# Pre-norm attention and expert block on one core: the query and key projections as three f32r products with split operands

## The reference, cut to what matters

```python
x = x + attn(layernorm(x))      # causal, window 128, 16 heads of 8
x = x + moe(layernorm(x))       # 16 experts, 4 chosen per token, and a shared one
# in attn:
qkv = x @ w_in.T + b_in         # the query and key parts of this are what changes
scores = einsum('bhqd,bhkd->bhqk', q, k) / sqrt(8), masked, softmax, @ v
return out @ w_out.T + b_out
```

## Time and profile before

| what | value |
|---|---|
| median of 3 runs (lowest to highest) | 761.21 us (756.61 to 762.22) |
| time of the profiled execution | 758.62 us |
| its span in the trace | 756.8 us |
| granted TensorE clock over the span | 0.972 |
| TensorE, matmul busy | 706.9 us (93%) |
| VectorE busy | 585.8 us (77%) |
| ScalarE busy | 362.4 us (48%) |
| GpSimd busy | 306.4 us (40%) |

### The profile page before, as it was taken

One profiled execution on the slowest core, in us unless ns is written; L12 is line 12 of the kernel. 1 busy time (PEld: TensorE's weight loads), 2 busy tenths in 40 slices (PEclk: granted clock), 3 DMA queues, 4 the chain that ended last, 5 costly groups with the idle time before them and its releaser, 6 DMA issues.

```text
span 756.8 us, 21746 instructions
## 1 busy us (share of the span) xinstructions
PE 706.9 (93%) x8499; PEld 472.2 (62%) x8499; DVE 585.8 (77%) x1741; ACT 362.4 (48%) x739; POOL 306.4 (40%) x327
## 2 busy tenths in 40 slices
PE   4597999999999999999778999999999999999997
PEld 2365666666666666666555666666666666666664
DVE  6776788888888888888577878887777888777632
ACT  2165566767776676667562332333333233333321
POOL 6410221222211222122215656566666656664543
PEclk9589899999999999999999999999999999999999
DMA  2125123333323222333118366654445666544550
GB/s 59 58 87 148 62 85 102 102 102 102 101 61 101 86 70 93 102 102 101 59 35 207 73 138 154 155 134 113 118 122 137 152 155 120 131 103 108 119 139 29
DMA packets 64837, 79.96 MB, mean 106 GB/s; under 512 B 10960, under 2 KB 38880, under 8 KB 64736
## 3 DMA queue, kind: packets, MB, share of 16 engines
q1 hardware_dynamic: 64736, 78.58, 39.9%
HBM read 61.00 MB, written 17.56 MB: 104 GB/s over the span
## 4 chain that ended last, share of the span: by engine, by line
PE 80%; DVE 7%; DMA 5%; ACT 4%; issue 2%; SPq 1%; POOL 1%; DVEq 0%; ACTq 0%; PEldq 0%
PE ps_c L1571 14%; PE ps_att L1356 7%; PE ps_sc L1330 6%; PE ps_max L1288 5%; PE ps_max L1560 4%; PE ps_max L1562 4%; PE ps_max L1561 4%; PE ps_sc L1306 4%; PE ps_sc L1561 4%; PE ps_sc L1562 4%; PE ps_sc L1560 4%; PE ps_a L1254 3%; ACT probs L683 3%; PE ps_c L1574 2%; PE ps_b L1247 2%
## 5 line engine op out<-in xcount | busy, mean ns | idle before, releaser
L618 POOL TENSOR_TENSOR probs<-probs,stacks 128x512 f32<-128x512 f32 x128 | 165.0, 1290 | 125.7 <-DVE probs L1105 75.4
L775 ACT ACTIVATE probs<-ps_max 128x512 f32<-128x512 f32 x144 | 86.2, 598 | 220.1 <-PE ps_max L1562 216.5
L886 DVE TENSOR_REDUCE chunkmax<-ps_max 128x16 f32<-128x512 f32 (+1 forms) x256 | 155.3, 648 | 37.9 <-PE ps_max L1269 37.8
L683 ACT ACTIVATE probs<-ps_sc 128x512 f32<-128x512 f32 x256 | 138.9, 595 | 48.6 <-PE ps_sc L1306 47.6
L1105 DVE TENSOR_TENSOR probs<-probs,ps_sc 128x512 f32<-128x512 f32 x128 | 87.3, 682 | 69.6 <-PE ps_sc L1562 26.4
L1571 PE MATMUL ps_c<-probs,wd 128*128 128x512 f32 x256 | 130.3, 592 | 1.3 <-POOL probs L618 1.3
L1560 PE MATMUL ps_max<-xh,whigh 128*128 128x512 f32 x144 | 93.7, 650 | 2.9 <-DVE probs L1105 2.1
L531 POOL TENSOR_TENSOR xres<-xin,cvec 128x512 f32<-128x512 f32 x16 | 20.6, 1287 | 141.1 <-DVE x L938 140.7
L1330 PE MATMUL ps_sc<-stacks 32*64 32x192 f16 (+2 forms) x2048 | 64.4, 232 | 9.5 <-ACT probs L683 2.7
L1356 PE MATMUL ps_att<-probs,stacks 128*32 128x192 f32 (+1 forms) x1536 | 70.2, 317 | 0.0
L1288 PE MATMUL ps_max<-hl,qdiag 32*128 32x160 f16 (+4 forms) x1024 | 50.9, 220 | 16.0 <-DVE chunkmax L886 9.7
(11 more groups left out here) (164 smaller groups left out, 1257.1 us busy)
## 6 DMA issues: line engine op xcount, KB each, us to landing
stacks<-weight_scratch SPq DMA_DIRECT2D x32, 1024.0 KB, 10.0
stacks<-qk_scratch SPq DMA_DIRECT2D x48, 256.0 KB, 3.4
qk_scratch<-hl SPq DMA_DIRECT2D x32, 256.0 KB, 3.4
xin<-in_L_attn_x_dram SPq DMA_DIRECT2D x16, 256.0 KB, 3.1
x_scratch<-x SPq DMA_DIRECT2D x16, 256.0 KB, 2.2
xin<-x_scratch SPq DMA_DIRECT2D x16, 256.0 KB, 8.9
xres<-x_scratch SPq DMA_DIRECT2D x16, 256.0 KB, 8.9
out_dram<-result SPq DMA_DIRECT2D x16, 256.0 KB, 8.8
```

The lines of the kernel that those rows point to most:

```text
L618: nc.gpsimd.tensor_tensor(inter[p % 3], gated[p % 2], spread[d % 2][:, p, :], ALU.mult).then_inc(inter_ready, 1)
L683: nc.scalar.activation(dst[:, :], ps_sc[s][:, 0:dst.shape[1]], ACT.Exp, scale=SCALE).then_inc(probs_ready, 1)
L775: nc.scalar.activation(silu[n % 2][rows, :], ps_max[n % 2][rows, :], ACT.Silu).then_inc(silu_ready, 1)
L886: nc.vector.tensor_reduce(chunkmax[:, 2 * pair + m, at:at + CHUNKS[h]], ps_max[m][:, 0:BANK_COLS[h]].rearrange("p (n k) -> p n k", k=KB), ...
```

## The change

Two pieces of split data are added: `xT` gets a high part `xT_high` and a low part `xT_low` (both 128x512, f32r), and the query and key weights get `wqk_high` and `wqk_low` (128x256, f32r). From step 1 on, a projection is the sum of three f32r products (high x high, low x high, high x low) in the same bank. Step 0 stays as it was. The parts are made so:

- ScalarE copies the transposed block a second time, from `ps_a` to `xT_high`, right behind the copy to `xT`. `project_v` now waits for this copy too.
- POOL subtracts `xT_high` from `xT` (`low_xT(i + 1)`), behind `layer_norm(i + 1)` and ahead of `residual(i + 1)`. TensorE waits for it in each of the two projections.
- Once, in `body(0)`, ScalarE copies the weights to `wqk_high` behind its copies of block 1. POOL makes `wqk_low` from it ahead of `other_constants`, and TensorE waits for it ahead of `body(1)`.

```diff
@@ POOL
+            def low_xT(d):
+                if not valid(d):
+                    return
+                pool.wait_ge(xT_high_ready, d)
+                after(pool, qk_done, 2 * d if d > 1 else 0)
+                nc.gpsimd.tensor_tensor(xT_low[:, :], xT[:, :], xT_high[:, :].bitcast(FP32), ALU.subtract
+                                        ).then_inc(xT_low_ready, 1)
+
+            def low_wqk():
+                pool.wait_ge(wqk_high_ready, 1)
+                nc.gpsimd.tensor_tensor(wqk_low[:, :, :], wT[:, 0:2, :], wqk_high[:, :, :].bitcast(FP32), ALU.subtract
+                                        ).then_inc(wqk_low_ready, 1)
             for i in range(STEPS):
                 residual(i)
                 if i == 0:
                     clear()
                 layer_norm(i + 1)
                 if i == 0:
+                    low_wqk()
                     other_constants()
+                low_xT(i + 1)
@@ ACT
                 nc.scalar.copy(xT[:, :], ps_a[:, :]).then_inc(xT_ready, 1)
+                if d > 0:
+                    nc.scalar.copy(xT_high[:, :], ps_a[:, :]).then_inc(xT_high_ready, 1)
...
                 transpose_out(prep + 1)
+                if prep == 0:
+                    act.wait_ge(wt_ready, 1)
+                    nc.scalar.copy(wqk_high[:, :, :], wT[:, 0:2, :]).then_inc(wqk_high_ready, 1)
                 take_att(now, 1)
@@ PE
-                mm((ps_b, ps_c)[n][:, :], wT[:, n, :], xT[:, :], start=True, stop=True).then_inc(qk_done, 1)
+                bank = (ps_b, ps_c)[n]
+                if d == 0:
+                    last = mm(bank[:, :], wT[:, n, :], xT[:, :], start=True, stop=True)
+                else:
+                    pe.wait_ge(xT_low_ready, d)
+                    mm(bank[:, :], wqk_high[:, n, :], xT_high[:, :], start=True, stop=False)
+                    mm(bank[:, :], wqk_low[:, n, :], xT_high[:, :], start=False, stop=False)
+                    last = mm(bank[:, :], wqk_high[:, n, :], xT_low[:, :], start=False, stop=True)
+                last.then_inc(qk_done, 1)
...
                 pe.wait_ge(xT_ready, d + 1)
+                after(pe, xT_high_ready, d)
...
             body(0)
             pe.wait_ge(consts2_ready, 1)
+            pe.wait_ge(wqk_low_ready, 1)
```

More of the change, by code:

```diff
@@ L105, in build_block @@
         xT = sb("xT", [P, TOK], FP32)
+        xT_high = sb("xT_high", [P, TOK], F32R)
+        xT_low = sb("xT_low", [P, TOK], F32R)
+        wqk_high = sb("wqk_high", [P, 2, P], F32R)
+        wqk_low = sb("wqk_low", [P, 2, P], F32R)
         hl = sb("hl", [P, 2, 2, TOK], FP16)
@@ L224, in build_block @@
         xT_ready = sem("xT_ready")
+        xT_high_ready = sem("xT_high_ready")
+        xT_low_ready = sem("xT_low_ready")
+        wqk_high_ready = sem("wqk_high_ready")
+        wqk_low_ready = sem("wqk_low_ready")
         qk_done = sem("qk_done")
```

## The result

The changed kernel took 766.75 us (median of 22 runs, 761.89 to 772.46), the kernel before 762.25 in 22 runs beside it (756.61 to 765.46): a ratio of 1.0064, 95% interval 1.0045 to 1.0084. The change costs 0.6%, where the prediction had 760.0 against the profiled execution of before, or 762.6 against the median shown. 766.75 lies outside both of its ranges (756.5 to 764, and 755 to 765.5 for 80%). That the ratio would be within 1% of no change was right, but the prediction held that less than about 1% couldn't be told from none, and 22 runs of each told 0.6%.

A forecast was written before the change was run, and what follows sets the result against it. It took ScalarE and then VectorE to hold the settled step, with projections as filler. From 758.62 us, +1.85 at the start and -0.5 in step 1 gave 760.0; own range 756.5 to 764, 80% range 755 to 765.5.

The forecast's parts named there:

- The projections are filler beside ScalarE's work: Settled attention step: `scores 2` and `scores 3` start 0.05 us behind ScalarE's exponentials, so the projections do not set the time.
- The shorter products: Projections on TensorE: three f32r products at 0.23 us replace one of 0.86, saving 0.16 us each, 4.8 over 15 steps.
- ScalarE's second copy: Behind the first copy in each step: ends 0.50 us later, taken as cost 0, bounds 0 and 0.1 a step.
- GpSimd's subtraction: `low_xT` in each step: 1.3 us long (bounds 1.0 and 2.6), 1.7 us of slack before `project_qk 0`, cost 0.
- VectorE held by the subtraction: Rival: GpSimd's subtraction slows VectorE or pushes L531 along `spread_q`, up to 0.94 us a step, 774 us; chance 0.04.
- The start, +1.85: `body(1)` on TensorE starts at 37.15 instead of 35.30 us, behind `low_wqk` and the constants; bounds 1.3 and 2.3.
- Step 1, -0.5: First step with f32r projections, at half clock and without `take_attn`: savings count, -0.5 us, ends -0.2 and -0.7.
- The clock "rises at the same moment / after as much work": TensorE's clock from `body(1)`: up to -0.9 us if same moment, 0 if after as much dense work; 0 taken.
- the zero case: TensorE's clock rises after as much dense work as before, adding 0 us.
- 0 for the 14 settled steps: Settled attention steps: ScalarE and then VectorE hold the step, so TensorE's savings gain 0; at most 0.6 us in all.
- the sum: Whole kernel: +1.85 us at the start, -0.5 in step 1, 0 in the settled steps, added to 758.62.
- the two 1% marks: Whole kernel: faster by over 1% (under 751 us) chance 0.02, slower by over 1% (over 768.8) chance 0.05.

The follow-up runs named there:

- h3: Changed kernel with projections left as one float32 product and four satisfied waits added in each projection; 766.53 us, ratio 1.0076 to the kernel before.
- h4: Kernel before with only the change's start: weight copy, `low_wqk` ahead of the constants and TensorE's wait; 761.12 us, ratio 1.0013.
- h2: Changed kernel run again unchanged, on another chip, against the kernel before; 769.08 us, ratio 1.0067.
- e1_same: Kernel before, nothing changed, against itself; 763.74 us, ratio 1.0013.
- h5: Kernel before with the change's start and sixteen satisfied waits more a step, nothing else of the change; 764.59 us, ratio 1.0053.
- g1: Changed kernel with `low_wqk` behind the constants, fewer waits, and 192 do-nothing instructions once in TensorE's `body(0)`; 760.53 us, ratio 0.9958 to the kernel before.
- g2: Changed kernel with `low_wqk` behind the constants and fewer waits, without the 192 do-nothing instructions; 771.13 us, ratio 1.0113 to the kernel before.
- h6: Kernel before with sixteen satisfied waits (eight instructions) more a TensorE step, repeated on another chip; 764.11 us, ratio 1.0042.
- h1: Kernel before with sixteen satisfied waits (eight instructions) more a TensorE step, first run; 764.78 us, ratio 1.0009.
- e2: Kernel before with the four new tensors allocated and not used; 764.21 us, ratio 1.0035.
- e4: Changed kernel with each projection left as one float32 product, the split operands made and not used; 772.24 us, ratio 1.010 to the kernel before.
- f1: Changed kernel with float32 projections, plus 192 do-nothing instructions once in TensorE's `body(0)`; 762.57 us, ratio 0.9966 to the kernel before.
- f4: Kernel before with 192 do-nothing instructions once in TensorE's `body(0)`; 766.42 us, ratio 1.0042.

## Why the prediction was wrong, step by step

- **"The projections are filler beside ScalarE's work"**: right. `scores 2` stands at 1.89 behind the transposes in both traces, and in on-time steps the step is 21.05 in both. h3 against after confirms it from the other side.
- **"The shorter products", 0.16 us each:** right (0.23 apart), and lost, as said.
- **ScalarE's second copy** at 0: right; it lasts 0.62 and ends at `take_att`'s start. **GpSimd's subtraction** at 1.3 us and no cost: right (1264 ns, mean of 15; 1.69 us of slack where 1.7 was worked out).
- **VectorE held by the subtraction:** did not happen; the two reductions beside it last 692 and 682 ns where they had 692 and 681, and the floor of the step is unchanged. The Trainium skill's "GPSIMD Engine Reference" (the table of its first section, row "SBUF interfaces") ties the contention to the kind of VectorE instruction. The trace agrees for these reductions, which read PSUM.
- **The start, +1.85:** nearly right, +2.10. GpSimd's row says why:

```profile
33.68 0.72 POOL L610 TENSOR_TENSOR wqk_low<-wT,wqk_high 128x256 fp32r<-128x256 f32 x1 [2.97 <-ACT wqk_high L763]
...
36.68 0.62 POOL L493 TENSOR_SCALAR_AFFINE_SELECT edges<-edges 64x64 bf16<-64x64 bf16 x2
```
```profile
37.40 0.64 PE L1369 MATMUL ps_sc<-stacks 32*64 32x192 f16 x12 [2.07 <-POOLq L587]
```

  TensorE waits 2.07 us for GpSimd. The subtraction took 0.72 (0.7 was estimated), the constants end at 37.30 (37.15), and 0.4 of the shift is not the change's at all: `spread_q` of step 0 took 7.50 us instead of 7.08, and all that follows was later. h4's start, 0.86 later than before, shows how much run-to-run movement lies in that term.
- **Step 1, -0.5:** about right. `scores 2` came 1.58 us behind the projection's start (42.22 - 40.64) where it was 2.00, 0.4 less; up to the anchor 0.3 of it were left.
- **The clock "rises at the same moment / after as much work":** taken as 0. Busy time by stretch, after and then before, of TensorE's time at the 1.2 GHz level (a clock of 0.50):

```profile
17.30:44.60 27.30, 14.21 (x175) 9.82 (x176) 19.50 (x51) 6.79 (x14) 12.62 (x23) 0.50 0.13 41
...
37.40:44.60 7.20, 7.20 (x73) 4.59 (x74) 3.64 (x15) 3.94 (x7) 3.14 (x6) 0.50 0.01 1
```
```profile
18.20:42.10 23.90, 13.80 (x173) 8.86 (x174) 17.40 (x47) 5.41 (x12) 10.17 (x21) 0.50 0.15 46
```

  It rose 2.5 us later with a `body(1)` that began 2.1 later, after 7.20 us of its work where before had 6.80: nearly the zero case. What the prediction did not price is the clock's next drop, in step 1: 6.8 us long in before (from 76.2) and 3.4 in after (from 78.8), part of the -1.7 there.
- **"0 for the 14 settled steps": this is the step that failed.** It took the 21.05 of the undisturbed steps as the length of all of them and asked only which engine sets it. The chain from one step to the next goes through SyncE's store and load of the row maxima, with about 0.5 us to spare, and I gave these no row and no price. The settled steps were 4.9 us above the floor in after and 8.4 in h2, where the sum says 0. The trace of before had the clue: two of its steps took 21.28 and 21.76 with round trips of 2.09 and 2.80. It then took an execution with 1.1 us of such delay as typical, where e1_same had 5.8. And none of the rivals had a price for the mere length of the code; h5 gives it, with the start, at 0.5%.
- **The last attention step had no term at all**, and so counted as 0. It was 2.1 us longer in after.
- **Where the time lies.** The sum had +1.35 us; 0.64% is 4.9. The mean span of after and h2 is 4.8 over that of before and e1, and of it +3.2 lie in the settled steps (excess 4.9 and 8.4 against 1.1 and 5.8), +3.3 in the last attention step, -1.7 in step 1, and nothing at the start, where h2's short `spread_q` hides the 2.1. Two traces each are few: the values of the settled steps overlap, those of the last attention step do not.
- **The range** from its own terms and 2 us of spread would be 755.7 to 764.2, not 756.5 to 764, and of the two 1% marks 751 is counted from the profiled execution and 768.8 from the median. Neither changes the outcome.

What is shown: satisfied waits alone move the time by 1.5% (g1 against g2, one chip); most long steps (82 of 102) have a late round trip of this store, and the longest of these trips have a 16 KB fetch beside the store in 45 of 47 cases; the start and a longer TensorE step alone give a ratio within the changed kernel's interval; the f32r products give nothing measurable. That the fetch holds the packets rests on packet times, in which the store's last packets come when the fetch is done.

What stays open: why a fetch 1.1 to 1.6 us behind the issue held some stores and not others, and the 0.6 us behind the last packet. Why the kernel before with the pad got slower is not explained, nor why one program's late steps differ from run to run. The split between start and code length is not settled: the intervals of h4, h6 and h5 overlap, and h1 and h6, one kernel, gave 1.0009 and 1.0042. Nor is it excluded that the copies and subtractions cost 0.2 to 0.3% (h3 against h5, h2 against the sum of h4 and the mean of h1 and h6). The layout (e2) could carry a part.

## What to carry to other kernels

Lay the lengths of the steps side by side before adding up engine times, and follow each small DMA on the chain from step to step: with 0.5 us of slack behind an 8 KB round trip, contention decides, and one lucky trace hides it. Look at the first and last steps too, where nothing is settled. Where a change's prize is below 1%, an edit that lengthens an engine's program is a rival with a price as large; repeat such a comparison at equal code length, with satisfied waits added on one side. Work saved in filler pays nothing, while preparing operands for it costs at the start, where nothing hides it.

## What the runs showed of the hardware that I had not expected

- Program fetches share the DMA engines with data: 68 or 69 packets of 16 KB a run, 0.9 to 2.0 us each. A store of 64-byte packets whose round trip is 1.42 us took 2.10 to 3.64 whenever one of them started within 1.1 us behind its issue, and a 256 KB load up to 5.5 us instead of 3.3.
- 192 instructions of satisfied waits, issued once, made one kernel 1.3% and another 1.5% faster (e4 to f1, g2 to g1), and the kernel before, if anything, slower (f4, 1.0042).
- Four 128x512 fp16 VectorE instructions beside GpSimd's early work took 3.77 or 7.50 us in two runs of one program.
- The granted clock fell to 0.50 for 3.4 us behind 14 of the 35 waits of TensorE of 1.0 us or more in the settled steps of the 18 traces.
